# The Mamba step size in a fused kernel: dt written to SBUF by VectorE, dt times x computed by GpSimd

## The chip, the core and the metric

One core of one Trainium2 chip runs the whole program. The metric is the device time of one execution in microseconds (us), shown as the median of several runs. Five engines run their own instruction streams and meet at semaphores: PE (TensorE, matrix products into PSUM), DVE (VectorE), ACT (ScalarE), POOL (GpSimd) and SP (SyncE, which here issues all DMAs).

## What is computed

Input is x of shape 8 x 96 x 64 x 64: 8 images of 4096 tokens with 96 channels. The first layer is a mixture of four experts with a router, applied to each token. The second is a bidirectional Mamba block; this is the part around the change:

```
xz = x @ W_in;  xr, z = split(xz)            # 192 channels each
xr = silu(conv(xr) + conv_b)
dbl = xr @ W_xproj
dt = softplus(dbl[..., :6] @ W_dt + b_dt)     # 192 channels
Bm, Cm = dbl[..., 6:22], dbl[..., 22:38]      # 16 states
A = -exp(A_log)
h = exp(dt * A) * h + (dt * x) * B            # for each token in turn, 192 x 16 states
y = sum over the states of h * C
y = (y + xr * D) * silu(z);  out = y @ W_out
```

It runs once over the tokens forward and once in reverse; the two outputs are averaged and added to the input of the block.

## The kernel before

Tokens are cut into chunks of CH = 512. A **body** works on one chunk in one direction: 8 forward and then 8 reverse bodies for each image, 128 in all. Bodies alternate between even and odd (`par`), with buffers for each. The 192 x 16 = 3072 states are 24 tiles of 128 rows. For tile i, ScalarE computes exp(dt*A) into one of three PSUM banks (`exp_dA`, L945, two tiles ahead), VectorE runs the recurrence with a scan instruction (`scan`, L1177), GpSimd multiplies four tiles at a time by C (`times_c`, L1256, behind a small copy of the last column, L1254), and TensorE sums over the states (`sum_states`, L709). The product (dt*x)*B is made in place before the scan: by GpSimd for batches 0 and 1 (`times_b`, L1246), by VectorE for batches 2 to 5 (`times_b`, L1161), whose B comes from PSUM through a ScalarE copy (`copy_b`, L933).

The order of each engine's work within a body is written out by hand, tied to the tile number i. VectorE waits for a copied B at i = 7, 11, 15 and 19. In a forward body ScalarE must first bring the finished y of the body before out of PSUM (`evacuate`, L950), and `copy_b` for i = 7 stands behind that in its queue. In a reverse body VectorE does the same job itself, by a product with silu(z) (`gate_y`, L1182).

The step size dt of the **next** chunk is made inside the current body. TensorE leaves the raw values in two PSUM banks, D1 (64 low channels, and B and C beneath them) and D0 (128 high channels). ScalarE computes abs, exp(-.) and log(1 + .) into SBUF (`LOG`, lines 910 to 916). VectorE then runs `make_dt` for the low half at i = 4 and for the high half at i = 6. It has two instructions: L1148 adds max(v, 0) and the logarithm and writes dt back into the PSUM bank v, and L1150 multiplies v by `xr` into SBUF. After that ScalarE copies dt from PSUM to SBUF (`copy_dt`, L926, at i = 5 and i = 7), over the logarithm, and this copy frees the bank. SP waits for that to store dt and dt*x to memory (`store_low`, `store_high`), from where they are read back in replicated form as `lo` and `hi` (`load_low`, `load_high`). Other work that feeds the next body hangs on TensorE: expert products, layer norm, the projection and `sum_states`, in a fixed order.

GpSimd's order in a body is: `times_c` for batches 0, 1 and 2, `times_b(n + 1, 0)`, in even bodies a layer norm product (L1227), `times_c` 3, `times_b(n + 1, 1)`, `times_c` 4 and 5. GpSimd runs late: `times_c` 5 of a body is done only while VectorE is at i = 3 to 6 of the next one.

Of the kernel before, what the change touches and what calls it, by code (L numbers as in the profile page):

```python
# [9 lines left out]
P = 128  # L10
# [5 lines left out]
DR = DI - P  # L16
# [192 lines left out]
def moe_mamba(nc, A):  # L209
# [3 lines left out]
    with ctx:  # L213
# [68 lines left out]
        S = sb("S", [P, 3, CH])  # L282
        bc = sb("bc", [P, CH])
# [35 lines left out]
        s_dt = [sem("dt_high_ready"), sem("dt_low_ready")]  # L319
# [62 lines left out]
        def _(sp):  # L382
# [19 lines left out]
            for credit in (s_x2s, s_xns, s_out, s_slo, s_sbc, *s_ys):  # L402
                sp.sem_inc(credit, 16)
            sp.sem_inc(s_shi, 32)
# [34 lines left out]
            def store_low(par, u):  # L439

                bank, at = u.at["D1"]
                wait_alone(s_pf[bank], at + 2)
                sp.dma_start(lo_d[par, :, :], S[:, 2, :]).then_inc(s_slo, 16)

# [5 lines left out]
            def store_high(par, u):  # L450
                bank, at = u.at["D0"]
                wait_alone(s_pf[bank], at + 2)
                for k in range(2):
                    sp.dma_start(hi_d[par, P * k:P * k + P, :], S[:, k, :]).then_inc(s_shi, 16)

# [15 lines left out]
            def load_low(b, par):  # L471
                wait_alone(s_slo, b * 16 + 32)
# [26 lines left out]
            _, _, _, rest, _ = prologue_uses()  # L499
# [4 lines left out]
            store_low(0, rest)  # L504
            store_high(0, rest)
# [26 lines left out]
            def body(img, q, rev, odd, head, last, before, p0, u, even, ahead):  # L532
# [19 lines left out]
                store_low(nxt, u)  # L552
# [11 lines left out]
                store_high(nxt, u)  # L564
# [261 lines left out]
        def _(act):  # L826
# [80 lines left out]
            def softplus_start(k, u, b):  # L907

                act.wait_ge((s_shi, s_slo)[k], b * (32, 16)[k] + (32, 16)[k])
# [12 lines left out]

            def copy_dt(k, u, b):

                act.wait_ge(s_dtx[k], b + 1)
                free(u, f"D{k}", A_(LOG[k], p_w[u.at[f"D{k}"][0]][0:ROWS_OF[k], :], ACT.Copy))  # L926
# [44 lines left out]
            copy_dt(1, rest, 0)  # L971
            copy_dt(0, rest, 0)
# [3 lines left out]
            def body(img, q, rev, odd, head, last, before, p0, u, even, ahead):  # L976
# [3 lines left out]
                for i in range(NT):  # L980
# [16 lines left out]
                    if i == 5:  # L997
                        copy_dt(1, u, n + 1)
# [35 lines left out]
        def _(dve):  # L1034
# [106 lines left out]
            DTX = (S[:, 1, :], S[DR:P, 2, :])  # L1141
            ROWS_OF = (P, DR)

            def make_dt(k, u, b, par):

                v = p_w[u.at[f"D{k}"][0]][0:ROWS_OF[k], :]
# [184 lines left out]
```

## Time and profile before

| | us |
|---|---|
| median of 3 runs | 6172.31 (6155.66 to 6182.67) |
| the profiled execution, its own time | 6168.89 |
| its span, first to last instruction | 6167.1 |
| VectorE busy in the span | 5465.0 (89%) |
| TensorE busy | 5041.7 (82%) |
| GpSimd busy | 4838.7 (78%) |
| ScalarE busy | 4444.7 (72%) |
| SyncE's queue, DMA share | 64.6% of 16 engines' span |
| granted TensorE clock, mean | 0.842 of full speed |

The first 400 us are set-up, router and first layer of the first image; the rest is the 128 bodies, which repeat with a period of one image (716.9 us, from 1124.9 to 1841.8 us). Reading it: no engine is busy all the time, and they wait for each other at a few fixed places of each body. The share of busy time says which engine could become the bound; which one is late at a place is said by the waits and the timeline.

### The profile page before, as it was taken

To read this page: it belongs to the slowest core of one execution; us is meant where nothing else is said; L and a number is where in the kernel's file an instruction comes from. 1 tells how busy PE (TensorE), PEld (TensorE's weight loads), DVE (VectorE), ACT (ScalarE), POOL (GpSimd) and SP (SyncE) were. 2 spreads that over 40 slices of the span, in tenths; PEclk is the share of its full clock that TensorE was granted. 3 is DMA by queue.
4 is the path that set the end of the run, shared out by engine and by line. 5 is a ranking of instruction groups with operands and counts; after the bars stand their busy time and mean duration, and the time that the engine had idled before them with its cause. 6 is when DMAs were issued, how large, how long until landed. Compare 5 with 4: busy or idle time off the path is not lost.

```text
span 6167.1 us, 69193 instructions
## 1 busy us (share of the span) xinstructions
PE 5041.7 (82%) x14273; PEld 1556.6 (25%) x14273; DVE 5465.0 (89%) x4732; ACT 4444.7 (72%) x6729; POOL 4838.7 (78%) x1869
## 2 busy tenths in 40 slices
PE   7768778888887788888888888888888888887887
PEld 7222222222222222222222222222222222222222
DVE  1239999999999999999999999999999999999998
ACT  0447777777777777777777777777777776777776
POOL 0038878888888888888888888888888887888887
PEclk9877889878888888887888788878888888887898
DMA  3046677666766666676666667676666766666766
GB/s 92 21 98 167 159 168 169 160 166 163 171 152 169 163 165 167 159 171 159 166 163 167 155 170 169 151 170 159 167 164 160 170 159 165 160 165 159 173 166 145
DMA packets 426299, 965.03 MB, mean 156 GB/s; under 512 B 56016, under 2 KB 56265, under 8 KB 392920
## 3 DMA queue, kind: packets, MB, share of 16 engines
q1 hardware_dynamic: 425944, 961.30, 64.6%
q14 instruction: 254, 2.08, 0.1%
q8 instruction: 101, 1.65, 0.1%
HBM read 776.98 MB, written 184.11 MB: 156 GB/s over the span
## 4 chain that ended last, share of the span: by engine, by line
PE 35%; issue 22%; DVE 20%; ACT 8%; DMA 7%; POOL 6%; SPq 2%; DVEq 1%; ACTq 0%; POOLq 0%
DVE X L1177 15%; PE ps L678 12%; PE ps L709 4%; POOL X L1256 3%; PE ps L700 3%; PE ps L657 2%; PE ps L703 2%; DMA lo_d<-S 2%; DVE X L1161 2%; PE ps L616 2%; DMA bc_d<-bc 2%; POOL X L1246 2%; DMA lo<-lo_d 1%; ACT L862 1%; ACT ps L945 1%
## 5 line engine op out<-in xcount | busy, mean ns | idle before, releaser
L1256 POOL TENSOR_TENSOR X<-X,cR 128x2048 f32<-128x2048 f32 x768 | 3477.7, 4528 | 61.8
L1177 DVE TENSOR_TENSOR_SCAN X<-ps,carry,X 128x512 f32<-128x512 f32 x2688 | 3260.5, 1266 | 76.6 <-ACT ps L945 63.9
L945 ACT ACTIVATE ps<-hi,amat 128x512 f32<-128x512 f32 x2048 | 1378.3, 684 | 880.4 <-DVE X L1177 876.7
L1161 DVE TENSOR_TENSOR X<-hi,ps 128x2048 f32<-128x2048 f32 x512 | 1165.0, 2275 | 216.1 <-PE ps L709 162.7
L1246 POOL TENSOR_TENSOR X<-lo,bR 128x2048 f32<-128x2048 f32 x258 | 1168.2, 4528 | 64.3 <-DMA lo<-lo_d 64.3
L709 PE MATMUL ps<-X,red 128*32 128x512 f32 x6144 | 930.5, 681 | 338.1 <-POOL X L1256 336.6
L678 PE MATMUL ps<-win,w_u 97*128 97x512 f32 (+1 forms) x2080 | 1200.8, 731 | 6.9 <-DMA win<-xn_d 5.9
L945 ACT ACTIVATE ps<-lo,amat 128x512 f32<-128x512 f32 x1026 | 697.5, 681 | 184.3 <-DVE X L1177 146.8
L1254 POOL COPY carry<-X 128x4 f32<-128x4 f32 x768 | 143.5, 187 | 859.3 <-DVE X L1177 853.2
L678 PEld LDWEIGHTS ps<-win,w_u 97*128 97x128 f32 (+1 forms) x2080 | 399.1, 203 | 715.3 <-issue 679.7
L693 PE MATMUL ps<-xr,wd 128*96 128x512 f32 (+1 forms) x520 | 373.8, 810 | 243.6 <-ACT xr L895 189.3
L641 PE MATMUL ps<-xp,w 96*128 96x512 f32 x864 | 520.7, 730 | 51.9 <-DMA xp<-in_x 37.8
L700 PE MATMUL ps<-xr,dg 64*128 64x512 f32 (+1 forms) x512 | 348.5, 767 | 145.8 <-DVE yr L1182 120.6
L1177 DVE TENSOR_TENSOR_SCAN X<-ps,X 128x512 f32<-128x512 f32 x384 | 443.2, 1204 | 27.2 <-POOL X L1246 19.4
L1138 DVE TENSOR_TENSOR hid<-ps,hid 128x512 f32<-128x512 f32 x432 | 290.0, 673 | 175.3 <-PE ps L648 174.6
L657 PE MATMUL ps<-hid,w 128*96 128x512 f32 x852 | 414.9, 607 | 0.0
L709 PEld LDWEIGHTS ps<-X,red 128*32 128x32 f32 x6144 | 126.4, 113 | 1024.8 <-POOL X L1256 647.8
L694 PE MATMUL ps<-xr,wd 65*96 65x512 f32 (+1 forms) x520 | 350.6, 764 | 0.0
L1227 POOL TENSOR_TENSOR xnp<-xc,sq 96x512 f32<-96x512 f32 x71 | 89.9, 1266 | 331.4 <-ACT sq L888 331.4
L853 ACT ACT_TABLE_LOAD x265 | 340.0, 1283 | 4.7
L933 ACT ACTIVATE ps<-bR 128x512 f32<-128x512 f32 x512 | 298.7, 583 | 0.0
L862 ACT ACTIVATE hid<-ps,b 128x512 f32<-128x512 f32 x432 | 269.3, 685 | 28.6 <-PE ps L641 26.6
(111 smaller groups left out, 4338.6 us busy)
## 6 DMA issues: line engine op xcount, KB each, us to landing
hi<-hi_d SPq DMA_DIRECT2D x516, 512.0 KB, 8.2
bR<-bc_d SPq DMA_DIRECT2D x516, 256.0 KB, 4.6
lo<-lo_d SPq DMA_DIRECT2D x516, 256.0 KB, 4.4
cR<-bc_d SPq DMA_DIRECT2D x516, 256.0 KB, 7.0
hi_d<-S SPq DMA_DIRECT2D x258, 256.0 KB, 7.9
lo_d<-S SPq DMA_DIRECT2D x129, 256.0 KB, 5.4
y_d<-yf SPq DMA_DIRECT2D x128, 256.0 KB, 8.2
yb<-y_d SPq DMA_DIRECT2D x128, 256.0 KB, 7.4
```

The costliest lines, as they stand in the source:

```text
L641: ready(u, f"H{m}", mm(begin(u, f"H{m}")[:, :], w1[:, P * m:P * m + P], xp[:, :], start=True, stop=True))
L657: mm(p_w[u.at["Y2"][0]][0:C, :], w2[:, m, :], hid[:, m, :], start=False, stop=False)
L678: last = mm(out[0:m, :], w_u[:, t, a:a + m], win[:, par, at:at + CH], start=(t == 0), stop=(t == TAPS - 1))
L693: mm(out[0:m, :], w_d[0][:, a:a + m], xr[0][:, par, :], start=True, stop=False)
L694: ready(u, name, mm(out[0:m, :], w_d[1][:, a:a + m], xr[1][:, par, :], start=False, stop=True))
L700: mm(p_y[:, :], diag[low][:, :], xr[low][0:(P, DR)[low], par, :], start=True, stop=False, skip_group_check=True)
L709: last = mm(p_y[GRP * j:GRP * j + GRP, :], red[:, :], X[:, slot(par, s), j, :], start=False, stop=(s in (LOW - 1, NB - 1)), skip_group_che ...
L945: A_(p_a[i % RING][:, :], dt, ACT.Exp, scale=amat[:, column(i):column(i) + 1]).then_inc(s_exp, 1)
L1161: V.tensor_tensor(X[:, slot(par, s), :, :], hi[:, par, HIGH:2 * HIGH, :], p_b[:, :].unsqueeze(1).to_broadcast([P, BATCH, CH]), ALU.mult).t ...
L1177: V.tensor_tensor_scan(h, a, h, 0.0 if head else carry[:, i:i + 1], ALU.mult, ALU.add).then_inc(s_scan, 1)
L1246: G.tensor_tensor(batch(par, s), lo[:, LOW:2 * LOW, :].unsqueeze(1).to_broadcast([P, 2, 2, CH]), quads(bR, par, s), ALU.mult).then_inc(s_b ...
L1256: G.tensor_tensor(batch(par, s), batch(par, s), quads(cR, par, s), ALU.mult).then_inc(s_hc, 1)
```

## The change

VectorE's first instruction (now `make_dt` alone) writes dt straight over the logarithm in SBUF, and its end frees the PSUM bank. ScalarE's two copies `copy_dt` are gone, with the two semaphores between. The product dt*x moves from VectorE to GpSimd as `times_x`, with both inputs in SBUF. It is called for the low half ahead of the first `times_c` of a body and for the high half behind it. The low product goes into rows 0 to 63 of `bc` instead of rows 64 to 127 of `S`, beside dt in rows 0 to 63 of `S`, and `store_low` becomes two DMAs of 128 KB instead of one of 256 KB. `store_low` and `store_high` now wait for GpSimd's product instead of ScalarE's copy.

```diff
@@ sync @@
-            def store_low(par, u):
-                bank, at = u.at["D1"]
-                wait_alone(s_pf[bank], at + 2)
-                sp.dma_start(lo_d[par, :, :], S[:, 2, :]).then_inc(s_slo, 16)
+            def store_low(b, par):
+                wait_alone(s_dtx[1], b + 1)
+                sp.dma_start(lo_d[par, 0:DR, :], S[0:DR, 2, :]).then_inc(s_slo, 16)
+                sp.dma_start(lo_d[par, DR:P, :], bc[0:DR, :]).then_inc(s_slo, 16)
...
-            def store_high(par, u):
-                bank, at = u.at["D0"]
-                wait_alone(s_pf[bank], at + 2)
+            def store_high(b, par):
+                wait_alone(s_dtx[0], b + 1)
...
             def load_low(b, par):
-                wait_alone(s_slo, b * 16 + 32)
+                wait_alone(s_slo, b * 32 + 64)
@@ scalar @@
-            def copy_dt(k, u, b):
-                act.wait_ge(s_dtx[k], b + 1)
-                free(u, f"D{k}", A_(LOG[k], p_w[u.at[f"D{k}"][0]][0:ROWS_OF[k], :], ACT.Copy))
...
                     if i == 5:
-                        copy_dt(1, u, n + 1)
                         copy_b(n, 0, par)
...
-                    if i == 7:
-                        copy_dt(0, u, n + 1)
-                        if not odd:
-                            ln_centred(u, pc - 1)
+                    if i == 7 and not odd:
+                        ln_centred(u, pc - 1)
@@ vector @@
-                V.scalar_tensor_tensor(v, v, 0.0, LOG[k], op0=ALU.max, op1=ALU.add).then_inc(s_dt[k], 1)
-                dve.wait_ge(s_dt[k], b + 1)
-                V.tensor_tensor(DTX[k], v, xr[k][0:ROWS_OF[k], par, :], ALU.mult).then_inc(s_dtx[k], 1)
+                free(u, f"D{k}", V.scalar_tensor_tensor(LOG[k], p_w[u.at[f"D{k}"][0]][0:ROWS_OF[k], :], 0.0, LOG[k],
+                                                        op0=ALU.max, op1=ALU.add))
@@ gpsimd @@
+            DT, DTX, ROWS_OF = (S[:, 0, :], S[0:DR, 2, :]), (S[:, 1, :], bc[0:DR, :]), (P, DR)
+            def times_x(k, u, par):
+                bank, at = u.at[f"D{k}"]
+                pool.wait_ge(s_pf[bank], at + 2)
+                G.tensor_tensor(DTX[k], DT[k], xr[k][0:ROWS_OF[k], par, :], ALU.mult).then_inc(s_dtx[k], 1)
...
+                times_x(1, u, nxt)
                 times_c(n, 0, par, rev)
+                times_x(0, u, nxt)
                 times_c(n, 1, par, rev)
```

On VectorE, around i = 3 to 7 of a body (in these listings a scan prints as SCALAR_TENSOR_TENSOR X<-ps, X), before:

```order
L1177 SCALAR_TENSOR_TENSOR X<-ps0,X 128x512
L1148 SCALAR_TENSOR_TENSOR ps6<-ps6,S 64x512
L1150 TENSOR_TENSOR S<-ps6,xr1 64x512
L1177 SCALAR_TENSOR_TENSOR X<-ps1,X 128x512
L1177 SCALAR_TENSOR_TENSOR X<-ps2,X 128x512
L1148 SCALAR_TENSOR_TENSOR ps7<-ps7,S 128x512
L1150 TENSOR_TENSOR S<-ps7,xr0 128x512
L1177 SCALAR_TENSOR_TENSOR X<-ps0,X 128x512
L1161 TENSOR_TENSOR X<-hi,ps3 128x2048
```

and now:

```order
L1163 SCALAR_TENSOR_TENSOR X<-ps0,X 128x512
L1135 SCALAR_TENSOR_TENSOR S<-ps6,S 64x512
L1163 SCALAR_TENSOR_TENSOR X<-ps1,X 128x512
L1163 SCALAR_TENSOR_TENSOR X<-ps2,X 128x512
L1135 SCALAR_TENSOR_TENSOR S<-ps7,S 128x512
L1163 SCALAR_TENSOR_TENSOR X<-ps0,X 128x512
L1147 TENSOR_TENSOR X<-hi,ps3 128x2048
```

Two instructions went from the row between the scans and the B product at i = 7.

On GpSimd, from the last `times_c` of one body over the start of the next, before:

```order
L1254 COPY carry<-X 128x4
L1255 REGISTER_ALU
L1256 TENSOR_TENSOR X<-X,cR 128x2048
L1252 ISA
L1254 COPY carry<-X 128x4
L1256 TENSOR_TENSOR X<-X,cR 128x2048
L1252 REGISTER_ALU
L1254 COPY carry<-X 128x4
L1255 REGISTER_ALU
L1256 TENSOR_TENSOR X<-X,cR 128x2048
```

and now:

```order
L1248 COPY carry<-X 128x4
L1249 REGISTER_ALU
L1250 TENSOR_TENSOR X<-X,cR 128x2048
L1220 REGISTER_ALU
L1221 TENSOR_TENSOR bc<-S,xr1 64x512
L1246 ISA
L1248 COPY carry<-X 128x4
L1250 TENSOR_TENSOR X<-X,cR 128x2048
L1220 REGISTER_ALU
L1221 TENSOR_TENSOR S<-S,xr0 128x512
L1246 REGISTER_ALU
L1248 COPY carry<-X 128x4
```

The two products stand on both sides of the body's first `times_c`, all ahead of its second.

In SP's queue of the same body, before:

```order
L461 DMA bR<-bc_d 32x2048 x4
L443 DMA lo_d<-S 128x512
L420 DMA xp<-in_x 96x512
L474 DMA lo<-lo_d 32x4x512 x4
L426 DMA x2_d<-x2p 96x512
```

and now:

```order
L461 DMA bR<-bc_d 32x2048 x4
L443 DMA lo_d<-S 64x512
L444 DMA lo_d<-bc 64x512
L421 DMA xp<-in_x 96x512
L474 DMA lo<-lo_d 32x4x512 x4
L427 DMA x2_d<-x2p 96x512
```

The store of the low half is two transfers; its place and that of all others is the same.

## Rows read from the trace of the kernel before

**Rows 1.** page, part 1: busy us (share of the span) and instructions of each engine

```profile
PE 5041.7 (82%) x14273; PEld 1556.6 (25%) x14273; DVE 5465.0 (89%) x4732; ACT 4444.7 (72%) x6729; POOL 4838.7 (78%) x1869
```

**Rows 2.** waits of the whole run: engine, line, releaser: us in total, times, longest

```profile
POOL carry L1254 <- DVE X L1177: 853.2, 288, 5.6
...
DVE X L1161 <- PE ps L709: 162.7, 101, 8.2
...
DVE X L1177 <- ACT ps L945: 71.3, 79, 4.4
...
DVE X L1161 <- ACT ps L933: 51.3, 70, 1.5
```

**Rows 3.** busy time by stretch: eight forward bodies, then eight reverse ones

```profile
1124.90:1472.60 347.70, 287.54 (x799) 81.43 (x792) 332.69 (x283) 270.59 (x410) 301.18 (x117) 0.80 0.69 166
1472.60:1841.80 369.20, 307.97 (x878) 92.81 (x880) 341.73 (x297) 272.05 (x414) 301.59 (x117) 0.87 0.67 162
```

**Rows 4.** groups by form: busy us, mean ns of one, idle before it

```profile
L1256 POOL TENSOR_TENSOR X<-X,cR 128x2048 f32<-128x2048 f32 x768 | 3477.7, 4528 | 61.8
...
L1227 POOL TENSOR_TENSOR xnp<-xc,sq 96x512 f32<-96x512 f32 x71 | 89.9, 1266 | 331.4 <-ACT sq L888 331.4
...
L1150 DVE TENSOR_TENSOR S<-ps,xr 128x512 f32<-128x512 f32 x129 | 89.2, 692 | 4.4
...
L926 ACT ACTIVATE S<-ps 128x512 f32<-128x512 f32 x129 | 74.7, 579 | 1.0 <-DVE S L1150 1.0
```

**Rows 5.** timeline of VectorE, a reverse odd body: start, us, instruction, idle before

```profile
3051.24 0.67 DVE L1148 SCALAR_TENSOR_TENSOR ps<-ps,S 64x512 f32<-64x512 f32 x1
...
3052.65 2.46 DVE L1177 TENSOR_TENSOR_SCAN X<-ps,carry,X 128x512 f32<-128x512 f32 x2
3055.03 0.67 DVE L1148 SCALAR_TENSOR_TENSOR ps<-ps,S 128x512 f32<-128x512 f32 x1
...
3056.34 0.68 DVE L1182 TENSOR_TENSOR yr<-ps,sz 128x512 f32<-128x512 f32 x1
...
3070.12 0.67 DVE L1182 TENSOR_TENSOR yr<-ps,sz 128x512 f32<-128x512 f32 x1
3070.70 1.28 DVE L1177 TENSOR_TENSOR_SCAN X<-ps,carry,X 128x512 f32<-128x512 f32 x1
```

**Rows 6.** timeline of GpSimd in the same body

```profile
3052.75 0.18 POOL L1254 COPY carry<-X 128x4 f32<-128x4 f32 x1
...
3061.75 0.19 POOL L1254 COPY carry<-X 128x4 f32<-128x4 f32 x1 [4.21 <-DVE X L1177]
```

**Rows 7.** timeline of all engines, start of a forward odd body

```profile
1981.71 0.18 POOL L1254 COPY carry<-X 128x4 f32<-128x4 f32 x1
...
1981.82 1.93 PE L709 MATMUL ps<-X,red 128*32 128x512 f32 x8 [3.66 <-POOL X L1256]
...
1983.82 0.60 ACT L950 ACTIVATE yf<-ps 128x512 f32<-128x512 f32 x1 [2.70 <-PE ps L709]
1984.31 0.58 ACT L926 ACTIVATE S<-ps 64x512 f32<-64x512 f32 x1
...
1984.79 0.59 ACT L933 ACTIVATE ps<-bR 128x512 f32<-128x512 f32 x1
...
1985.50 2.29 DVE L1161 TENSOR_TENSOR X<-hi,ps 128x2048 f32<-128x2048 f32 x1 [1.43 <-ACT ps L933]
...
1989.15 0.19 POOL L1254 COPY carry<-X 128x4 f32<-128x4 f32 x1 [2.65 <-DVE X L1177]
```

**Rows 8.** timeline of all engines, a reverse even body

```profile
3018.41 0.60 ACT L880 ACTIVATE xf<-ps 96x512 f32<-96x512 f32 x1 [0.84 <-PE ps L720]
...
3028.21 1.28 DVE L1177 TENSOR_TENSOR_SCAN X<-ps,carry,X 128x512 f32<-128x512 f32 x1 [0.53 <-ACT ps L945]
```

**Rows 9.** timeline of SyncE's queue, the first reverse body of an image

```profile
2206.22 1.74 SPq L474 DMA_DIRECT2D lo<-lo_d  x4
```

**Rows 10.** timeline of VectorE in that first reverse body

```profile
2231.74 2.29 DVE L1161 TENSOR_TENSOR X<-hi,ps 128x2048 f32<-128x2048 f32 x1 [8.04 <-PE ps L709]
```

More of the change, by code:

```diff
@@ L318, in moe_mamba @@
         s_sp = [sem("softplus_steps_high"), sem("softplus_steps_low")]
-        s_dt = [sem("dt_high_ready"), sem("dt_low_ready")]
         s_dtx = [sem("dtx_high_ready"), sem("dtx_low_ready")]
@@ L401, in _ @@
             ]
-            for credit in (s_x2s, s_xns, s_out, s_slo, s_sbc, *s_ys):
+            for credit in (s_x2s, s_xns, s_out, s_sbc, *s_ys):
                 sp.sem_inc(credit, 16)
-            sp.sem_inc(s_shi, 32)
+            for credit in (s_slo, s_shi):
+                sp.sem_inc(credit, 32)
             for out, src in loads:
@@ L498, in _ @@
             pad(NCH - 1)
-            _, _, _, rest, _ = prologue_uses()
             sp.wait_ge(s_pad, 16 * (2 + PIX // 1024) * IMGS)
@@ L503, in _ @@
             store_bc(0, 0)
-            store_low(0, rest)
-            store_high(0, rest)
+            store_low(0, 0)
+            store_high(0, 0)
             load_b(0, 0)
@@ L551, in body @@
                 load_b(n + 1, nxt)
-                store_low(nxt, u)
+                store_low(n + 1, nxt)
                 if not odd:
@@ L563, in body @@
                 load_c(nxt)
-                store_high(nxt, u)
+                store_high(n + 1, nxt)
                 if before == 0:
@@ L907, in softplus_start @@
             def softplus_start(k, u, b):
-                act.wait_ge((s_shi, s_slo)[k], b * (32, 16)[k] + (32, 16)[k])
+                act.wait_ge((s_shi, s_slo)[k], b * 32 + 32)
                 A_(LOG[k], begin(u, f"D{k}")[0:ROWS_OF[k], :], ACT.Abs).then_inc(s_sp[k], 1)
@@ L970, in _ @@
                 softplus_log(k, 0)
-            copy_dt(1, rest, 0)
-            copy_dt(0, rest, 0)
             for i in range(LEAD):
@@ L1140, in _, with make_dt @@
             LOG = (S[:, 0, :], S[0:DR, 2, :])
-            DTX = (S[:, 1, :], S[DR:P, 2, :])
             ROWS_OF = (P, DR)
-            def make_dt(k, u, b, par):
-                v = p_w[u.at[f"D{k}"][0]][0:ROWS_OF[k], :]
+            def make_dt(k, u, b):
                 dve.wait_ge(s_sp[k], b * 3 + 3)
-                V.scalar_tensor_tensor(v, v, 0.0, LOG[k], op0=ALU.max, op1=ALU.add).then_inc(s_dt[k], 1)
-                dve.wait_ge(s_dt[k], b + 1)
-                V.tensor_tensor(DTX[k], v, xr[k][0:ROWS_OF[k], par, :], ALU.mult).then_inc(s_dtx[k], 1)
+                free(u, f"D{k}", V.scalar_tensor_tensor(LOG[k], p_w[u.at[f"D{k}"][0]][0:ROWS_OF[k], :], 0.0, LOG[k],
+                                                        op0=ALU.max, op1=ALU.add))
             def times_b(n, h, par):
@@ L1191, in _ @@
             for k in (1, 0):
-                make_dt(k, rest, 0, 0)
+                make_dt(k, rest, 0)
             def body(img, q, rev, odd, head, last, before, p0, u, even, ahead):
@@ L1199, in body @@
                     if i == 4:
-                        make_dt(1, u, n + 1, nxt)
+                        make_dt(1, u, n + 1)
                     if i == 6:
-                        make_dt(0, u, n + 1, nxt)
+                        make_dt(0, u, n + 1)
                         if fin:
@@ L1260, in _ @@
                 normalise(j)
+            _, _, _, rest, _ = prologue_uses()
+            for k in (1, 0):
+                times_x(k, rest, 0)
             for s in range(LOW):
```

## The prediction

> **What bounds the kernel now.** I read the busy shares first. VectorE is busy 89% of the span, ahead of TensorE (82%) and GpSimd (78%) [rows 1]. A share over the whole run hides where it is late, so next come the stretches: eight forward bodies take 347.7 us with VectorE busy 332.7, eight reverse bodies 369.2 us with 341.7 busy [rows 3]. So VectorE idles 15.0 / 8 = 1.9 us in a mean forward body of 43.5 us, and 27.5 / 8 = 3.4 us in a reverse one of 46.1 us. It is nearly the bound, but something else ends last at a few places of most bodies. The waits say what [rows 2]: VectorE's B product waits for TensorE's `sum_states` (162.7 us) and for ScalarE's `copy_b` (51.3 us, 70 times), its scan for ScalarE's exponential (71.3 us). GpSimd waits for VectorE's scans for 853.2 us, or 6.7 us a body: that is the room for new work there, if it lies where the work is put. The timeline tells where each wait lies in a body [rows 5 to 8, 10].
>
> **VectorE: two products leave.** A step of `make_dt` takes the time from its start to the start of what follows. The low half takes 3052.65 - 3051.24 = 1.41 us, the high half 3056.34 - 3055.03 = 1.31 us [rows 5]. One instruction of this size alone takes 3070.70 - 3070.12 = 0.58 us to the next [rows 5], although its own duration is 0.67. What is left is one such instruction for each half, so VectorE saves 2.72 - 2 x 0.58 = 1.56 us a body. The result now goes to SBUF and not to PSUM; L1150 has just such inputs and output and means 692 ns [rows 4], against 0.67 for L1148 [rows 5], so this costs 0 to 0.02 us each. I take **1.54 us a body**, or 197 us over 128 bodies, if all of it reached the end.
>
> **GpSimd: two products arrive.** No such product of 512 columns runs there in the bodies except the layer norm's, 96 x 512, at 1.27 us [rows 4]. From below, a quarter of L1256 (four times the columns) is 4.53 / 4 = 1.13 us; from above I take half of L1256, 2.26 us. I use 1.27, since columns and both-inputs-in-SBUF are the same and only rows differ. That is 2.54 us a body. Is it hidden? The low product stands between the last `times_c` of the body before and the first of this one, the high one behind that. The second `times_c` waits for scan 7. In a reverse odd body the first `times_c` starts at 3052.75 (nothing idle ahead of it) and the second at 3061.75, after 4.21 us of waiting [rows 6]. Those 9.00 us must now hold 4.8 + 2.54 = 7.3 us, while scan 7 comes 1.54 us earlier, leaving 7.46: it just fits. In a forward odd body the room is 1989.15 - 1981.71 = 7.44 us with 2.65 waited [rows 7]; scan 7 comes up to 1.5 us earlier there, so GpSimd can be late by 7.3 - (7.44 - 0.5) = 0.4 us or more, once a body. From `times_c` 2 on it waits again for scan 11, whose place VectorE sets. So I cost the arrival at 0 in reverse bodies and about 0.3 us in forward ones.
>
> A rule of the Trainium skill speaks against the move: GPSIMD Engine Reference, Engine selection, gives elementwise two-input work to VectorE because GpSimd is about 2 times slower at it. The trace agrees in kind (1.27 against 0.69 us [rows 4]). By that rule alone the change trades 1.54 us for 2.54; it would lose about 1 us a body only if GpSimd had no room.
>
> **ScalarE: two copies leave** (0.58 us each [rows 4]). It mostly waits, so this counts only where a copy stands in a chain. That is in forward bodies: GpSimd ends the last `times_c` (1981.71), TensorE sums (1981.82), `evacuate` (1983.82), the dt copy (1984.31), `copy_b` (1984.79), and VectorE's B product starts at 1985.50 after waiting 1.43 us [rows 7]. Without the copy this chain is 1984.79 - 1984.31 = **0.48 us** shorter. VectorE arrives 1.54 us earlier and waits that much more, except for these 0.48 us.
>
> **SP:** one more DMA issue in `store_low`, 0.3 to 0.6 us until the load of `lo` can start behind it. Its waits for ScalarE's copies become waits for GpSimd's products. Counted from the end of GpSimd's last `times_c` at 1981.71, the low copy ended 1984.31 + 0.58 - 1981.71 = 3.2 us later [rows 7] and the low product will end 1.3 us later; the high product ends 7.3 us later. Behind these waits in the queue stand the loads of `lo`, C and `hi` for the next body, for which no engine waits in [rows 2]. The exception is the first reverse body of an image, where y of the forward pass is stored and reloaded behind them, the `lo` load starting at 2206.22 [rows 9], and VectorE waits 8.04 us at 2231.74 [rows 10]. That stretch hangs on DMA, so VectorE's gain vanishes in it and I add 0.4 us.
>
> **The sum, for one image of 16 bodies:**
> - 4 reverse odd bodies: no long wait stands behind the saving, so 4 x 1.54 = 6.2 us.
> - 3 reverse even bodies and the image's first: scan 14 waits 0.53 us for ScalarE (3028.21), which had waited for TensorE's output product (3018.41) [rows 8]. TensorE's path through the experts is not shortened, so an earlier VectorE only waits longer. 4 x 0.15 = 0.6.
> - the first reverse body: -0.4.
> - 7 forward bodies: 4 with the `copy_b` wait (70 such waits in 128 bodies [rows 2]) gain 0.5 each; 3 without it gain 1.54 less what the chain and GpSimd then hold back, 1.0 each. Together 5.0.
>
> 11.4 us an image, 91 us for 8 images, less 1 us for the products that now lie bare at the start. The profiled execution took 6168.9 us, so it would take 6079; the median of the runs is 3.4 us above it, so I predict **6082 us**, 1.5% faster.
>
> **Rivals.**
> 1. *Most of the saving reaches the end.* TensorE's granted clock has two levels, 1.2 and 2.4 GHz, and the mean was 0.80 in the forward stretch against 0.87 in the reverse one [rows 3]. If shorter waits for VectorE kept it at the upper level more often, the waits for `sum_states` would shrink along with the saving. 1.2 us x 128 = 154: **6018 us**. For it: part of the sums run slow today (1.93 us after 3.66 idle [rows 7]). Against: this wait is for GpSimd and stays. Chance 0.12.
> 2. *Other chains hold nearly everything.* Only the reverse odd bodies gain, and what they gain is taken back partly in the even body behind, which hangs on TensorE. 4 x 0.8 x 8 = 26: **6147 us**. For it: VectorE's 162.7 us of waiting for TensorE [rows 2] show how close that path lies. Chance 0.18.
> 3. *GpSimd becomes the bound: slower.* The mechanism is one place, the second `times_c` of a body, on which TensorE's next sum, the projection behind it and so VectorE's last B product hang. In forward bodies the room of 7.44 us less 4.8 leaves 1.3 us for each product before that place is later than today, and about 1.6 before the loss exceeds what was saved. At the upper bound of 2.26 us it would be 4.8 + 4.52 - 7.44 = 1.9 us late; less 0.5 of slack, 1.4 x 56 forward bodies = 78 us lost and nothing gained in the reverse ones: **6250 us**. Against it: the 1.27 us of the layer norm product. Chance 0.09.
> The Trainium skill's SBUF page (Who interferes with whom) adds that a VectorE instruction with two SBUF inputs would block GpSimd's reads. VectorE's remaining step has one input in PSUM, so by that rule nothing is added; no row shows the other case.
> 4. *The change doesn't do what it says*, in that VectorE's single step stays as long as the two because of the switch between memories: within 20 us of today, **6172 us**. L1150 speaks against it. Chance 0.01.
>
> **Chances.** The forecast, 6045 to 6120, has 0.60. The range must take in most of rivals 1 and 2: 6010 to 6150 leaves out the far part of rival 1 (0.04), rivals 3 and 4 and a little of 2. A measurement of this kernel can tell about 0.5%, 31 us, from no change. Faster by more than that, below 6141: 0.60 + 0.12 + 0.05 of rival 2 = 0.77. Within it: 0.13 of rival 2, 0.01 of rival 4 and 0.01 of a mild rival 3 = 0.15. Slower: 0.08.
>
> **What would show it.** In the profile after: L1135 at about 0.67 us with scans 0.6 us behind it, or the first term is wrong; `times_x` at 1.2 to 1.3 us, or the second. GpSimd's wait at the second `times_c` falls from 2.6 to 4.2 us to nearly nothing, and its busy time rises by 258 x 1.27 = 328 us. VectorE's wait for `copy_b` grows to about 1 us more in forward bodies. Reverse odd bodies shorten by 1.5 us, even ones hardly: if both shorten alike, the TensorE chain was not the hold I take it for. The first reverse body still waits about 8 us or more. The prediction is wrong if the wait for `sum_states` grows past 300 us (rival 2) or GpSimd's `times_c` 2 no longer waits for a scan (rival 3).

## The result, and the profile after

| | before | after |
|---|---|---|
| median, us | 6168.0 (4 runs, 6155.66 to 6182.67) | 6060.82 (4 runs, 6058.65 to 6065.3) |
| span of the profiled execution, us | 6167.1 | 6063.5 |

The changed kernel is 1.7% faster: ratio 0.9827, 95% interval 0.981 to 0.9845. The medians here and below leave out the few executions that took far longer than the others of their kernel (9562.53 us for the unchanged copy, 10723.87 us for the kernel with two stores).

The page after, part 1, answers [rows 1]:

```profile
PE 4967.7 (82%) x14273; PEld 1536.1 (25%) x14273; DVE 5276.6 (87%) x4474; ACT 4307.0 (71%) x6471; POOL 5156.9 (85%) x2127
```

VectorE lost 188 us of busy time, GpSimd gained 318. The waits of the whole run after (engine, line, releaser: us in total, times, longest), against [rows 2]:

```profile
POOL carry L1248 <- DVE X L1163: 413.3, 226, 7.8
...
DVE X L1147 <- PE ps L708: 133.7, 68, 9.7
DVE X L1147 <- ACT ps L927: 107.8, 73, 2.5
...
DVE X L1163 <- ACT ps L939: 81.7, 99, 2.9
DVE yr L1168 <- PE ps L708: 75.2, 43, 9.2
```

GpSimd's wait for scans halved (853.2 to 413.3): its 318 us of new work lie in it, and the span is 104 us shorter. VectorE's wait for `copy_b` doubled (51.3 to 107.8).

The groups by form (busy us, mean ns of one, idle before it) give the sizes of the new instructions:

```profile
L1221 POOL TENSOR_TENSOR S<-S,xr 128x512 f32<-128x512 f32 x129 | 164.3, 1273 | 0.7 <-DVE S L1135 0.7
L1221 POOL TENSOR_TENSOR bc<-S,xr 64x512 f32<-64x512 f32 x129 | 164.0, 1271 | 61.8 <-DVE S L1135 60.7
...
L1135 DVE SCALAR_TENSOR_TENSOR S<-ps,S 128x512 f32<-128x512 f32 x129 | 85.4, 662 | 1.3 <-ACT S L915 1.3
```

VectorE's timeline in a reverse body (start, us, instruction) shows what stands in place of [rows 5]:

```profile
2310.55 0.66 DVE L1135 SCALAR_TENSOR_TENSOR S<-ps,S 64x512 f32<-64x512 f32 x1
2311.14 2.44 DVE L1163 TENSOR_TENSOR_SCAN X<-ps,carry,X 128x512 f32<-128x512 f32 x2
2313.50 0.66 DVE L1135 SCALAR_TENSOR_TENSOR S<-ps,S 128x512 f32<-128x512 f32 x1
2314.08 0.68 DVE L1168 TENSOR_TENSOR yr<-ps,sz 128x512 f32<-128x512 f32 x1
```

0.59 and 0.58 us from start to the next, where it was 1.41 and 1.31. GpSimd's timeline around it, as [rows 6] before:

```profile
2311.91 1.28 POOL L1221 TENSOR_TENSOR bc<-S,xr 64x512 f32<-64x512 f32 x1
2313.13 0.19 POOL L1248 COPY carry<-X 128x4 f32<-128x4 f32 x1
2313.40 4.54 POOL L1250 TENSOR_TENSOR X<-X,cR 128x2048 f32<-128x2048 f32 x1
2317.89 1.28 POOL L1221 TENSOR_TENSOR S<-S,xr 128x512 f32<-128x512 f32 x1
2319.49 0.19 POOL L1248 COPY carry<-X 128x4 f32<-128x4 f32 x1 [0.32 <-DVE X L1163]
```

The second `times_c` still waits for a scan, now 0.32 us instead of 4.21: it just fits. Over the 112 bodies of images 2 to 8 the wait at that place fell from 3.3 to 0.3 us in the mean forward body and from 4.7 to 0.9 in the mean reverse one; 44 of them no longer wait there.

**Where the time went.** I cut images 2 to 8 into stretches, each body counted from its low `make_dt` to the next one. A sum row of such windows gives us, then the busy time of each engine. The six reverse bodies behind the first, before (42 bodies):

```profile
sum 1935.22, PE 1635.78 PEld 496.51 DVE 1805.97 ACT 1432.96 POOL 1585.36; mean PE 233.68 PEld 70.93 DVE 258.00 ACT 204.71 POOL 226.48
```

and after:

```profile
sum 1866.93, PE 1608.31 PEld 485.26 DVE 1741.22 ACT 1388.20 POOL 1683.08; mean PE 229.76 PEld 69.32 DVE 248.75 ACT 198.31 POOL 240.44
```

VectorE's busy time fell by 64.75 us, which is 1.54 x 42, and the stretch by 68.3. The two sums are nearly equal; whether the one is made of the other is asked below, body by body. The eight forward bodies, before and then after:

```profile
sum 2443.88, PE 1995.13 PEld 563.29 DVE 2328.87 ACT 1894.10 POOL 2105.62; mean PE 285.02 PEld 80.47 DVE 332.70 ACT 270.59 POOL 300.80
```

```profile
sum 2414.13, PE 1960.26 PEld 555.88 DVE 2250.01 ACT 1833.69 POOL 2245.33; mean PE 280.04 PEld 79.41 DVE 321.43 ACT 261.96 POOL 320.76
```

Here VectorE saved 78.9 us and the stretch 29.8, 0.53 us a body: two thirds turned into waits. In the first reverse body the seven windows together grew from 338.47 to 353.26 us, 2.1 us each. For an image the change is -9.8 us in the six reverse bodies, -4.2 forward, +2.1 in the first reverse and -0.6 in the last: -12.5 us.

### The profile page after: what moved, and what is told of

Same layout as the page of the kernel before. It is cut to its first block, busy times and chain, and to the rows that moved or that the text cites. A ratio compares the mean times of both kernels' runs of the same rounds, so it can differ in the third digit from the quotient of the medians.

```text
span 6063.5 us, 68824 instructions
## 1 busy us (share of the span) xinstructions
PE 4967.7 (82%) x14273; PEld 1536.1 (25%) x14273; DVE 5276.6 (87%) x4474; ACT 4307.0 (71%) x6471; POOL 5156.9 (85%) x2127
## 3 DMA queue, kind: packets, MB, share of 16 engines
q14 instruction: 247, 2.02, 0.1%
## 4 chain that ended last, share of the span: by engine, by line
issue 25%; PE 25%; DVE 14%; DMA 10%; POOL 9%; ACT 7%; SPq 2%; DVEq 1%; ACTq 0%; POOLq 0%
DVE X L1163 11%; PE ps L677 8%; POOL X L1250 4%; DMA bc_d<-bc 3%; PE ps L708 3%; POOL X L1240 3%; DMA lo_d<-bc 3%; DMA lo<-lo_d 2%; PE ps L699 2%; PE ps L702 2%; PE ps L656 2%; ACT ps L939 1%; DVE X L1147 1%; PE ps L717 1%; DMA y_d<-yf 1%
## 5 line engine op out<-in xcount | busy, mean ns | idle before, releaser
L1147 DVE TENSOR_TENSOR X<-hi,ps 128x2048 f32<-128x2048 f32 x512 | 1164.6, 2275 | 244.6 <-PE ps L708 133.7
L677 PE MATMUL ps<-win,w_u 97*128 97x512 f32 (+1 forms) x2080 | 1112.7, 684 | 5.9 <-DMA win<-xn_d 4.8
L677 PEld LDWEIGHTS ps<-win,w_u 97*128 97x128 f32 (+1 forms) x2080 | 369.7, 188 | 669.5 <-issue 634.5
L1248 POOL COPY carry<-X 128x4 f32<-128x4 f32 x768 | 144.5, 188 | 417.6 <-DVE X L1163 413.3
L1127 DVE TENSOR_TENSOR hid<-ps,hid 128x512 f32<-128x512 f32 x432 | 289.8, 673 | 176.1 <-PE ps L647 174.9
```

The source lines that it names most:

```text
L677: last = mm(out[0:m, :], w_u[:, t, a:a + m], win[:, par, at:at + CH], start=(t == 0), stop=(t == TAPS - 1))
L1147: V.tensor_tensor(X[:, slot(par, s), :, :], hi[:, par, HIGH:2 * HIGH, :], p_b[:, :].unsqueeze(1).to_broadcast([P, BATCH, CH]), ALU.mult).t ...
```

## The experiments

Two theories stood first. **A**: VectorE's time is what pays. **B**: the copies and their chain pay. Line numbers in the rows are those of each kernel.

### VectorE's time given back

The changed kernel, with VectorE's second instruction of each half run again for nothing in the PSUM bank, where [rows 5] had it:

```diff
-                free(u, f"D{k}", V.scalar_tensor_tensor(LOG[k], p_w[u.at[f"D{k}"][0]][0:ROWS_OF[k], :], 0.0, LOG[k],
-                                                        op0=ALU.max, op1=ALU.add))
+                v = p_w[u.at[f"D{k}"][0]][0:ROWS_OF[k], :]
+                V.scalar_tensor_tensor(LOG[k], v, 0.0, LOG[k], op0=ALU.max, op1=ALU.add).then_inc(s_dt[k], 1)
+                dve.wait_ge(s_dt[k], b + 1)
+                free(u, f"D{k}", V.tensor_tensor(v, v, xr[k][0:ROWS_OF[k], par, :], ALU.mult))
```

> The changed kernel, with VectorE's second product run again for nothing (it writes v times xr into the PSUM bank and then frees the bank; GpSimd's product is the one that is used). VectorE has its old time back, ScalarE's copies stay away, GpSimd keeps its two products. Theory A, VectorE's 1.54 us a body are what paid: 80 us or more come back, 6140 to 6170 us. Theory B, the gain came from ScalarE's missing copies and the earlier free bank: at most 20 us come back, 6060 to 6080 us.

Measured: 6146.55 us, ratio to before 0.9986 (0.9973 to 0.9998), where the unchanged copy of the changed kernel, run beside it, gave 6057.49, ratio 0.9843 (0.9819 to 0.9868).

> The changed kernel once more, as the base of its company. Every theory expects 6061 us (6055 to 6070), 107 us under the kernel before.

So 88 us by the ratios, 89 by the medians, come back with VectorE's time: nearly all of the gain. This edit also frees the PSUM bank one product later; the next kernel frees it later still and bounds what that can cost. The six reverse bodies are back at their old length:

```profile
sum 1932.06, PE 1632.81 PEld 495.85 DVE 1800.61 ACT 1390.21 POOL 1686.99; mean PE 233.26 PEld 70.84 DVE 257.23 ACT 198.60 POOL 241.00
```

### The copies run for nothing

```diff
+            def copy_dt(k, u, b):
+                v = p_w[u.at[f"D{k}"][0]][0:ROWS_OF[k], :]
+                act.wait_ge(s_dt[k], b + 1)
+                free(u, f"D{k}", A_(v, v, ACT.Copy))
...
+                        copy_dt(1, u, n + 1)
...
+                        copy_dt(0, u, n + 1)
```

> The changed kernel, with ScalarE's two copies run again for nothing at their old places (bank to itself, freeing the bank as before); GpSimd's product waits for VectorE alone. Theory A: the copy stands only in the forward chain to copy_b, 0.48 us in some 50 bodies, so 15 to 30 us come back, 6075 to 6090 us. Theory B: most of the 107 us come back, 6130 us or more.

Measured: 6071.46 us, ratio 0.9859 (0.9836 to 0.9883). That is 10 us above the copy of the changed kernel by the ratios and 14 by the medians, with intervals that overlap: the two ScalarE copies and the later bank are worth 10 to 14 us together, if anything. VectorE's wait for `copy_b` did grow, from 107.8 to 142.9 us. Theory B falls.

### The product kept on VectorE, from two SBUF inputs

The changed kernel without the move to GpSimd: VectorE writes dt to SBUF and multiplies there.

```diff
+                bank, at = u.at[f"D{k}"]
+                dve.wait_ge(s_pf[bank], at + 2)
+                V.tensor_tensor(DTX[k], LOG[k], xr[k][0:ROWS_OF[k], par, :], ALU.mult).then_inc(s_dtx[k], 1)
...
-                times_x(1, u, nxt)
...
-                times_x(0, u, nxt)
```

> The changed kernel, with the product made by VectorE again, now from dt and xr both in SBUF; no copies, nothing new on GpSimd. Theory A: VectorE's time is back and GpSimd has its room, so about as the kernel with VectorE's time back or up to 15 us less, 6125 to 6165 us, with the product at 0.69 us. Theory C, by the Trainium skill's SBUF page (Who interferes with whom): a VectorE instruction with two SBUF inputs waits for GpSimd's reads, which fill most of the time in pieces of 4.5 us; then the product takes 2 us or more on the average, and with 256 of them the time is 6300 us or more.

Measured: 6508.61 us, ratio 1.0561 (1.0542 to 1.058), much slower than both. Its groups by form:

```profile
L1141 DVE TENSOR_TENSOR bc<-S,xr 64x512 f32<-64x512 f32 x129 | 307.1, 2381 | 4.5
L1141 DVE TENSOR_TENSOR S<-S,xr 128x512 f32<-128x512 f32 x129 | 251.3, 1948 | 4.5
L1253 POOL COPY carry<-X 128x4 f32<-128x4 f32 x768 | 190.0, 247 | 1153.2 <-DVE X L1168 1145.6 <-DMA cR<-bc_d 5.7 <-issue 1.8
```

The same product takes 2.38 and 1.95 us in place of 0.69, or (2.38 + 1.95 - 1.38) x 128 = 378 us in all; the kernel took 362 us more than the one with VectorE's time given back, which has one input in PSUM (and GpSimd's two products besides). Its timeline (VectorE and GpSimd) shows why:

```profile
3014.99 4.53 POOL L1255 TENSOR_TENSOR X<-X,cR 128x2048 f32<-128x2048 f32 x1
3017.52 0.65 DVE L1137 SCALAR_TENSOR_TENSOR S<-ps,S 64x512 f32<-64x512 f32 x1
3018.21 1.86 DVE L1141 TENSOR_TENSOR bc<-S,xr 64x512 f32<-64x512 f32 x1
3019.47 0.65 POOL L1253 COPY carry<-X 128x4 f32<-128x4 f32 x1
...
3020.20 4.51 POOL L1255 TENSOR_TENSOR X<-X,cR 128x2048 f32<-128x2048 f32 x1
...
3023.05 2.20 DVE L1141 TENSOR_TENSOR S<-S,xr 128x512 f32<-128x512 f32 x1
```

The first product ends at 3020.07, 0.55 us behind the end of GpSimd's running instruction (3014.99 + 4.53 = 3019.52); the second at 3025.25, 0.54 us behind its end (3024.71). Each ends only when GpSimd is done and a product's own length has gone by, and GpSimd's next copy, caught in turn, takes 0.65 us instead of 0.19. The Trainium skill, SBUF — State Buffer, Who interferes with whom, has this: a VectorE instruction with two SBUF inputs and a GpSimd one that reads SBUF exclude each other for the length of the instruction. These rows agree with it. So dropping the PSUM round trip alone, without the move, would have lost 5.6%: that part of the change needs the other. (The move with the round trip kept was not run.)

### How much room GpSimd has

The changed kernel with each GpSimd product done twice:

```diff
+                G.tensor_tensor(DTX[k], DT[k], xr[k][0:ROWS_OF[k], par, :], ALU.mult).then_inc(s_dx1[k], 1)
+                pool.wait_ge(s_dx1[k], b + 1)
                 G.tensor_tensor(DTX[k], DT[k], xr[k][0:ROWS_OF[k], par, :], ALU.mult).then_inc(s_dtx[k], 1)
```

> The changed kernel, with each of GpSimd's two products made twice (2.54 us more a body, at the same places). Theory A, GpSimd's second times_c is by now at the edge in forward and close to it in reverse bodies: most of what is added reaches the end, 100 to 250 us, 6160 to 6310 us, slower than before the change. Theory D, GpSimd still has its room (it waits 413 us for VectorE's scans): under 40 us, below 6100 us.

Measured: 6139.54 us, ratio 0.9945 (0.9925 to 0.9964): about 75 us more than after by the spans (6138.4 against 6063.5), 63 to 73 by the ratios to before, for 2.54 x 128 = 325 us of new work. Its waits say where it went:

```profile
DVE hid L1128 <- PE ps L648: 249.5, 111, 16.4
...
POOL carry L1251 <- DVE X L1164: 146.6, 95, 7.8
```

GpSimd's wait at the second `times_c` is gone: one body in 112 still has it. VectorE waits 75 us more for TensorE's gate product (174.9 after, 174.6 before), which stands in TensorE's order behind sums that wait for GpSimd. By stretches the eight forward bodies are at 2472.37 us, 58 above after; the six reverse ones at 1878.70, 12 above.

The opposite, with only 16 of the 512 columns multiplied (0.22 us for each product):

> The changed kernel, with GpSimd's two products cut to their first 16 columns; dt times x is otherwise left out, so the states are wrong past them. It shows what the arrival on GpSimd costs. Theory A: 0.3 us in forward bodies and 0 in reverse ones as predicted, so about 20 us, 6035 to 6050 us. Theory D: nothing, 6055 to 6065 us. Theory E, the hold at the second times_c is much more than predicted: under 6010 us.

Measured: 6055.73 us, ratio 0.9805 (0.9786 to 0.9824). By the medians that is 2 to 5 us under the changed kernel and its copy, by the ratios to before 14 to 23, with intervals that overlap: the products as the change has them cost some 20 us of the 328 that they take, or nothing. The run can't tell the 17 us predicted (0.3 us in 56 forward bodies) from none. Nor does it pay to move the high product behind the second `times_c`:

> The changed kernel, with the high product behind GpSimd's second times_c instead of ahead of it. Theory A: that times_c starts up to 1.27 us earlier, which frees the forward bodies of half of GpSimd's hold: 5 to 30 us less, 6030 to 6055 us. Rival: the later store of the high half (4.8 us) runs into the loads behind it in SyncE's queue, above all in the first reverse body, 6065 to 6090 us.

Measured: 6055.22 us, ratio 0.9818 (0.9793 to 0.9843), not told apart from the change.

### Why the reverse bodies gave everything

I had said that a reverse even body hangs on TensorE, which an earlier VectorE doesn't shorten. Before, TensorE's clock was low there behind a wait for ScalarE. TensorE's timeline before, in body 12 of an image (counted from 0, so reverse and even):

```profile
2399.63 0.39 PE L648 MATMUL ps<-gT,gsel 12*128 12x512 bf16 x1 [1.49 <-ACT hid L862]
2400.21 0.60 PE L648 MATMUL ps<-gT,gsel 12*128 12x512 bf16 x1 [0.19 <-ACT hid L862]
2400.74 6.71 PE L678 MATMUL ps<-win,w_u 97*128 97x512 f32 x8
```

The mean granted clock over the eight records was 0.55 of full speed. After, the same eight took 3.70 us at a granted clock of 1.00 in the body that answers to it, and VectorE's mean wait for the sum behind them went from 2.0 to 0.8 us.

By the time of these eight records, the 21 reverse even bodies 10, 12 and 14 of images 2 to 8 fall into three kinds. Each entry has the number of bodies and their length in us:

| eight records | before | after | its unchanged copy | VectorE's time back |
|---|---|---|---|---|
| 6.7 to 7.0 us | 18 (48.0 to 48.8) | 1 (48.7) | 0 | 15 (47.9 to 48.7) |
| 5.4 us | 1 (45.6) | 11 (45.5 to 45.6) | 6 (45.5 to 45.6) | 2 (45.5) |
| 3.7 us | 2 (45.1) | 9 (42.8 to 45.1) | 15 (42.8 to 45.1) | 4 (45.1 to 46.5) |

A body of one kind is mostly as long after as before, although VectorE has 1.5 us less to do in it. Body 10 of images 2 and 3, a slow one and a fast one, as rows of windows (length; busy time of PE, PEld, DVE, ACT and POOL; granted clock), first before, then after:

```profile
1569.44:1618.10 48.66, 43.02 (x133) 13.15 (x131) 43.04 (x39) 35.68 (x56) 39.63 (x16) 0.93 0.66 163
2289.22:2334.31 45.09, 40.65 (x125) 12.41 (x127) 42.96 (x39) 35.62 (x56) 38.48 (x16) 0.92 0.71 174
```

```profile
1556.12:1604.79 48.67, 43.02 (x133) 13.14 (x131) 41.58 (x36) 34.66 (x54) 42.12 (x18) 0.93 0.65 162
2265.46:2310.55 45.09, 40.46 (x125) 12.29 (x127) 41.47 (x36) 34.58 (x54) 41.10 (x18) 0.92 0.71 174
```

In the slow pair VectorE's first wait in the body took all that had been saved; its later waits are the same to 0.01 us. Timeline of VectorE, before and then after:

```profile
1575.98 0.69 DVE L1182 TENSOR_TENSOR yr<-ps,sz 128x512 f32<-128x512 f32 x1 [1.36 <-PE ps L709]
```

```profile
1562.67 0.69 DVE L1168 TENSOR_TENSOR yr<-ps,sz 128x512 f32<-128x512 f32 x1 [2.94 <-PE ps L708]
```

So within one kind an earlier VectorE does only wait longer. What the change altered is how many bodies are of the slow kind. An estimate from the table: with the lengths of before and the shares of after a mean even body takes 45.5 us; before it took 47.8 and after 45.0, so about 2.3 of the 2.8 us come with the shares. It rests on three fast bodies before. The 42.8 us bodies stand in no row before; in them some of VectorE's own saving may have arrived. The last column says that VectorE's time sets the shares: with it back, the slow kind is back, as it is (20 of 21) in the kernel before with two stores, further down. How it does that is not shown.

Was the low clock at that one place the lever? The kernel **before**, with one of the four taps put into the 1.49 us of waiting:

```diff
+                early = int(rev == 1 and not odd)
+                if early:
+                    pe.wait_ge(s_win[par], windows)
+                    project(0, par, urev, u, range(1))
                 gate_rows(rows, u, even)
                 gate_rows(rows + 1, u, even)
...
+                project(0, par, urev, u, range(early, TAPS))
```

> The kernel before, with one thing else: in reverse even bodies TensorE does the first of the four taps of the projection of the high half ahead of the two gate products instead of behind them. Nothing is added; the tap fills a part of the 1.5 us in which TensorE waits there for ScalarE's gelu. In the profile of before, the eight matmul records behind that wait took 6.71 us at the lower clock; after the change the same eight took 3.70 us. Theory E (reverse even bodies gained 2 to 3 us each from the change because TensorE kept the upper clock there): the projection takes 3.7 us in all, VectorE's wait for the sum behind it goes, and the bodies 10, 12 and 14 of an image shrink from 48 to about 45.5 us without any change on VectorE: 3 x 2.5 x 8 = 60 us less than before, about 6110. Theory F (the bodies gained because VectorE had less to do, and the clock only followed): the tap saves at most the 0.9 us that it moves into the gap, 0 to 20 us less, 6150 to 6170.

Measured: 6171.35 us, ratio 0.9997 (0.9987 to 1.0007). As theory E had it, with this one place as the cause, it falls. The edit did what it should at its place, and it was given back at the next. TensorE's timeline in such a body:

```profile
2407.79 1.13 PE L678 MATMUL ps<-win,w_u 97*128 97x512 f32 x2 [0.91 <-ACT hid L868]
2408.85 0.60 PE L648 MATMUL ps<-gT,gsel 12*128 12x512 bf16 x2
2409.38 2.84 PE L678 MATMUL ps<-win,w_u 97*128 97x512 f32 x6
...
2423.09 2.07 PE L684 MATMUL ps<-win,w_g 97*128 97x512 f32 x2 [3.00 <-ACT xr L901]
2425.92 2.02 PE L694 MATMUL ps<-xr,wd 128*96 128x512 f32 x2 [0.76 <-ACT sz L906]
2427.73 1.91 PE L695 MATMUL ps<-xr,wd 65*96 65x512 f32 x2
```

The taps took 1.13 + 2.84 us instead of 6.71, and VectorE's last B product didn't wait. But then TensorE waited 3.00 us for ScalarE's silu, which stands in ScalarE's queue behind exponentials that wait for VectorE's scans. Behind that idle time the granted clock was 0.50 to 0.52, its lower level, and the pairs took 2.02 and 1.91 us where they had taken 1.09 and 1.02. VectorE's scan then waited 1.80 us for an exponential. The six reverse bodies:

```profile
sum 1931.90, PE 1644.98 PEld 499.96 DVE 1804.25 ACT 1430.31 POOL 1584.27; mean PE 235.00 PEld 71.42 DVE 257.75 ACT 204.33 POOL 226.32
```

3.3 us less over 42 bodies. TensorE's busy time there didn't fall but rose, from 1635.78 to 1644.98 us, where the change had brought it down to 1608.31. So this run shows that keeping the clock up in one gap gives nothing by itself. It doesn't test a TensorE that is faster in the whole body, and the table above leaves that as the way on which most of the gain of the even bodies arrived.

In the odd bodies another wait stands close behind the saving. After, VectorE waits there for `copy_b` at i = 11, 1.2 us in the mean (1.31 in the body shown above), behind TensorE's output group at the lower clock (0.57 from 2314 to 2322 us). Behind an even body of 48.7 us the odd one took 44.1 us before and 43.2 after, behind one of 45.1 us 44.3 and 45.2. The changed kernel, with that group's first product, which doesn't need the gated y, put ahead:

```diff
+                if fin and odd:
+                    finish_begin(u, finished(img, q, rev, odd)[2])
                 y_begin(1, n, f, par)
                 if not odd:
                     ln_mean(u)
+                if fin and not odd:
+                    finish_begin(u, finished(img, q, rev, odd)[2])
```

> The changed kernel, with one thing else: the first product of TensorE's output group (the residual, which needs only data from memory and a free bank) goes ahead of the sum's opening product in reverse odd bodies, behind the layer norm's mean in even ones, and no longer waits for the gated y. In odd bodies the group took three pairs of 1.9 us each at the lower clock, behind VectorE's gate of y, and copy_b of i = 11 stood behind it on ScalarE: VectorE's wait there grew from 0.3 to 1.2 us with the change. Theory G (this chain is what took 0.8 us of the 1.54 us from each reverse odd body): one pair of 1.9 us leaves the chain, the wait for copy_b goes, and the four odd bodies shorten by 0.8 to 1.2 us each: 4 x 1 x 8 = 30 us less than the changed kernel, about 6030. Theory H (the next wait stands close behind it, or the pair is only moved to a place where it delays the sum): within 10 us of the changed kernel, 6050 to 6070.

Measured: 6077.66 us, ratio 0.9848 (0.9825 to 0.9871), no gain; a small loss can't be told from none. The product now stood ahead of its data:

```profile
2310.24 2.02 PE L716 MATMUL ps<-xf,ident 96*96 96x512 f32 x2 [1.12 <-DMA xf<-x_d]
```

Such waits sum to 41.3 us (32 times, up to 3.7). This test doesn't speak for or against the chain; it put a DMA in its place.

### SP's queue and the first reverse body

The kernel before, with the low store as two DMAs:

```diff
-                sp.dma_start(lo_d[par, :, :], S[:, 2, :]).then_inc(s_slo, 16)
+                sp.dma_start(lo_d[par, 0:DR, :], S[0:DR, 2, :]).then_inc(s_slo, 16)
+                sp.dma_start(lo_d[par, DR:P, :], S[DR:P, 2, :]).then_inc(s_slo, 16)
```

> The kernel before, with the store of the low half issued as two DMAs of 128 KB instead of one of 256 KB; nothing else. It prices that step of the change alone. All theories: one more issue in SP's queue each body, 0.3 to 0.6 us; it can only count in the first reverse body of an image, where VectorE waits for a chain of DMAs: 0 to 5 us more than before, not distinguishable from it. Over 20 us more would mean that SP's queue is close to the path in other bodies too.

Measured: 6177.62 us, ratio 1.001 (0.9993 to 1.0028). The second store is free within what can be told.

In the first reverse body after, the whole chain of [rows 9, 10] is still there. Timeline of all engines:

```profile
2201.54 2.08 PE L702 MATMUL ps<-yb,ident 128*128 128x512 f32 x2 [5.97 <-DMA yb<-y_d]
...
2209.35 2.29 DVE L1147 TENSOR_TENSOR X<-hi,ps 128x2048 f32<-128x2048 f32 x1 [7.86 <-PE ps L708]
```

The load of `yb` waits for the store of the forward y, and that store stands in SP's queue behind `store_high`, which now waits for GpSimd's high product. The changed kernel with this store ahead of it, behind `store_low`, in that one body:

```diff
                 store_low(n + 1, nxt)
+                if before == 0 and rev:
+                    store_y(0, n - 1, NCH - 1)
...
                 if before == 0:
-                    store_y(0, n - 1, NCH - 1 if rev else q * 2 + odd - 1)
+                    if not rev:
+                        store_y(0, n - 1, q * 2 + odd - 1)
```

> The changed kernel, with the store of the forward pass's last high y put ahead of the loads of lo and C and of the store of the high half in SyncE's queue, in the first reverse body of each image alone; its reload stays behind them. Theory: VectorE's wait of 8 us there ends with that reload, which can start some 7 us earlier: 40 to 60 us less, 6000 to 6020 us. Rival: the reload is late for its place in the queue, not for the landing of the store: under 15 us less.

Measured: 6034.81 us, ratio 0.9774 (0.9754 to 0.9794): the fastest of all, 2.3% under before. Under the changed kernel it lies by 26 us by the medians and by 33 to 43 by the ratios to before. The seven first reverse bodies sum to 319.78 us, 4.8 less each than after. VectorE's timeline in one of them shows what is late now:

```profile
2176.41 0.69 DVE L1171 TENSOR_TENSOR yr<-ps,sz 128x512 f32<-128x512 f32 x1 [5.67 <-PE ps L711]
...
2189.99 2.29 DVE L1150 TENSOR_TENSOR X<-hi,ps 128x2048 f32<-128x2048 f32 x1 [2.20 <-PE ps L711]
```

The wait at the B product shrank from 7.86 to 2.20, and one for the low sum of 5.67 stands ahead of it. Ahead of the first of these rows, at 2168.99, TensorE had waited 3.51 us for the DMA of `xp`, so this body still waits for DMA, for another transfer.

With the tap and the residual product added to it:

> The changed kernel with three edits of order together: the store of the forward high y ahead in SP's queue in the first reverse body (worth about 30 us alone), the first tap ahead of the gate products in reverse even bodies, and the residual product ahead in the output group. If the three stretches are independent, as different bodies and waits suggest, their gains add: 30 for the first, 20 to 30 for the third, and 0 to 20 for the second (in the changed kernel the clock fell behind that gap only in some of the even bodies, which then take 45.5 to 48.6 us instead of 42.8): 5980 to 6010. If they share one slack, it stays near 6030.

Measured: 6080.29 us, ratio 0.9852 (0.983 to 0.9873). The gains don't add; 45 us are lost against the early store alone. The reverse odd bodies 11, 13 and 15 took 46.6 to 47.6 us in the mean, 3 more than after, the even ones 43.6 to 44.3, about one less. TensorE's timeline, a reverse odd body:

```profile
2407.86 2.02 PE L720 MATMUL ps<-xf,ident 96*96 96x512 f32 x2 [3.93 <-DMA xf<-x_d]
```

The residual ahead of its data holds up TensorE by 3.93 us, and VectorE then waited 4.34 us for `copy_b`. No run has the early store and the tap without the residual, so what each of the two did to the sum is read from such rows alone.

## Why the prediction was right, and where it was not

The time, 6082, is 21 us above the measured median, within the range, and the forecast of the likeliest case (6045 to 6120) held. The terms of VectorE and GpSimd were right; that the sum over the bodies came out close is in good part luck. For an image, against the sum, the reverse odd bodies gave 4.2 us less, the reverse even ones 8.0 more, the forward bodies with the image's first 0.9 less and the first reverse body 1.7 less: 12.5 in place of 11.4. By its steps:

- **VectorE, 1.54 us a body**: right. Busy time fell by 64.75 us in 42 reverse bodies, exactly 1.54 each.
- **GpSimd, 1.27 us a product**: right (1.27), and nearly hidden: between nothing and some 20 us come back without it. The second `times_c` of the body shown still waits for a scan, 0.32 us, as the 7.3 against 7.46 us had it.
- **Forward bodies**: 4.2 us an image measured in eight bodies, 5.0 + 0.15 predicted. The chain through `evacuate` and `copy_b` takes part of the rest: 1.2 to 2.0 us of `copy_b` wait in the mean forward odd body, where it was 0.4 to 1.5. The gain is unevenly spread: the image's first body took 43.3 us in place of 42.0, bodies 4 and 6 gained 2.0 each. What I named as the gain there, the 0.48 us of the copy in 32 bodies, would be 15 us; with the copies back it was 10 to 14 in all, not clear of noise.
- **Reverse odd bodies, 4 x 1.54**: not as said. They shortened by 0.1 to 1.1 us in the mean (44.77 to 43.70 in the first), 2.0 us an image together, while VectorE waited 0.9 us more at the `copy_b` of i = 11.
- **Reverse even bodies, 0.15 each**: wrong. They shortened by 1.8 to 3.6 us (48.21 to 44.64), 8.4 us an image for three. The step that failed is the first half of "TensorE's path through the experts is not shortened, so an earlier VectorE only waits longer". The second half held: a slow body took 48.66 us before and 48.67 after, with 1.58 us more of waiting. But TensorE's path did get shorter, without an edit to it: its eight records took 6.7 us or more in 18 of 21 bodies before and in 1 after. The prediction had this as rival 1, at 0.12, and took the clock as fixed in its sum. It came in part: VectorE's wait for `sum_states` fell from 162.7 to 133.7 us, and the estimate above makes 2.3 x 3 x 8 = 55 us of it.
- **First reverse body, +0.4**: its sign was right, its size not: +2.1. The high product ends late, as counted (7.3 us against 3.2), and the forward y is stored behind it. I had priced the DMA issue, not this wait; the early store then gave 4.8 us a body.
- **Rival 3** (GpSimd the bound): its place was right, its price far too high. At twice the work, 2.54 us for each product, the second `times_c` no longer waits and the forward bodies are 0.5 us longer than before, but the whole kernel took 6139.54 us, still under before, where the rival had 6250 at 2.26 us.
- **The Trainium skill** (GPSIMD Engine Reference, Engine selection) gives elementwise work to VectorE, since GpSimd is about 2 times slower at it. The trace agrees on the speed (1.27 against 0.69 us); the move paid all the same, because GpSimd had been waiting at its place.
- **The Trainium skill's rule on two SBUF inputs** (SBUF — State Buffer, Who interferes with whom): the prediction left it outside the sum, rightly, since the remaining instruction has an input in PSUM. Its price stood in no row before; the kernel that meets it took 6508.61 us, 5.6% more than before.

What stays open: how VectorE's time changes the share of slow bodies. TensorE's granted clock was higher in the reverse bodies after (0.89 to 0.90 in those windows, 0.87 to 0.88 before); no run here held VectorE's time fixed and made TensorE faster in a whole body. Also open is what the output group's chain is worth in odd bodies, as the one test of it brought in a DMA.

## What to carry to other kernels

Before you take the mean of a body's length, sort the bodies by how the engine on the path ran in them. Here the mean reverse even body gained 2.8 us although bodies of one kind mostly gained nothing: fewer were slow. A wait can be slack in each body and the kernel still gain, so a sum over waits needs a term, with a chance, for the clock of another engine that an edit may shift.

Keeping the clock up in one gap of a steady loop gave nothing here (ratio 0.9997); look at the busy time of the engine over the whole stretch before you call it faster.

When work moves to another engine, ask where its operands lie. An elementwise product may be slower there and still pay if it lies in that engine's wait; kept on VectorE with both inputs in SBUF beside a busy GpSimd, it took about three times its length here (2.38 and 1.95 us against 0.69).

When an instruction is placed ahead in a queue, look at its latest input: the early store gained 4.8 us in each first reverse body, while the early residual product made TensorE wait for a DMA, up to 3.7 us, and gained nothing.

## What the runs showed of the hardware

- VectorE's 128 x 512 product with two SBUF inputs took 1.95 us in the mean, with one in PSUM 0.69, beside GpSimd products of 4.53 us. It ended 0.54 and 0.55 us behind the end of the running GpSimd instruction. GpSimd's 0.19 us copy took up to 0.67 in that kernel and at most 0.21 before and after.
- GpSimd's product of 512 columns took 1.27 us with 64, 96 and 128 rows alike; with 16 columns 0.22, with 2048 4.53.
- TensorE's granted clock didn't follow the idle time ahead of it in a fixed way: behind waits of 1.5 and 0.19 us the same eight records took 6.71 us at a mean granted clock of 0.55 in one body and 3.70 us at 1.00 in another (the levels are 1.2 and 2.4 GHz). In the kernel with the tap ahead, the same taps took 1.13 + 2.84 us, and the slow records (granted clock 0.50 to 0.52) stood behind the next wait, which had grown from none to 3.00 us.
- In the four traces of the table, the length of a reverse even body went with the time of these eight records, with or without VectorE's 1.54 us: 47.9 to 48.8 us at 6.7 us and more, 45.5 to 45.6 at 5.4, 42.8 to 46.5 at 3.7. With the early store the slow kind is less uniform: five such bodies took 44.6 to 48.8 us.
